# Weight quantisation prologue of an FFN-attention-FFN kernel: the loads for the mean scan move from ScalarE's queue to SyncE's, and the scale is folded and spread by TensorE instead of through DRAM

## What is computed

```python
def _weight_quant(w):
    scale = 1.0 / jnp.clip(jnp.mean(jnp.abs(w)), 1e-05)
    wq = jnp.clip(jnp.round(w * scale), -1.0, 1.0) / scale
    return w + jax.lax.stop_gradient(wq - w)
...
gate = jax.nn.silu(_bitlinear(x, w_gate))      # w_gate, w_up: 4096 x 1024
up = _bitlinear(x, w_up)
return _bitlinear(gate * up, w_down)           # w_down: 1024 x 4096
...
x = x + 0.5 * _L0_ffn_ref(_layernorm(x, axis=-1), w_gate, w_up, w_down)
x = x + _L0_attn_ref(_layernorm(x, axis=-1), w, u, mix_k, mix_v, mix_r, Wk, Wv, Wr, Wo)
x = x + 0.5 * _L0_ffn_ref(_layernorm(x, axis=-1), w_gate, w_up, w_down)
```

## Time and profile before

| | us |
|---|---|
| median of 2 timed runs | 8868.89 (8834.52 and 8903.26) |
| profiled execution, its own time | 8818.1 |
| its span on the slowest core (core 3) | 8816.5 |
| spans of the eight cores | 8726.9 to 8816.5 |
| TensorE, VectorE, ScalarE busy, core 3 | 3563.4, 2656.1, 1360.8 |

### The profile page before, as it was taken

One profiled execution on the slowest core, in us unless ns is written; L12 is line 12 of the kernel. 1 busy time (PEld: TensorE's weight loads), 2 busy tenths in 40 slices (PEclk: granted clock), 3 DMA queues, 4 the chain that ended last, 5 costly groups with the idle time before them and its releaser, 6 DMA issues.

```text
span 8816.5 us, 50500 instructions; the slowest of 8 cores (8726.9 to 8816.5 us)
## 1 busy us (share of the span) xinstructions
PE 3563.4 (40%) x15872; PEld 1586.1 (18%) x15872; DVE 2656.1 (30%) x2719; ACT 1360.8 (15%) x2012; POOL 687.6 (8%) x572
## 2 busy tenths in 40 slices
PE   0000435342464435342464435342464435442464
PEld 0000112131121112131121112131121112231121
DVE  0312131275302131275302132275302132275302
ACT  1221101021110101022110101021110101021110
POOL 0000101000110101000110101000110101000110
PEclk9999978776898778766798778766798778766797
DMA  7799432500243333501243322501243332501243
GB/s 171 205 229 197 132 85 90 129 1 29 85 115 91 122 85 93 124 1 37 80 122 86 124 82 93 122 1 38 82 118 86 124 85 92 119 1 48 80 121 96
DMA packets 1010045, 842.29 MB, mean 96 GB/s; under 512 B 639865, under 2 KB 902012, under 8 KB 990076
## 3 DMA queue, kind: packets, MB, share of 16 engines
q1 hardware_dynamic: 970768, 620.94, 28.4%
q10 hardware_dynamic: 29676, 167.79, 5.2%
q0 software_dynamic: 9344, 50.34, 2.2%
HBM read 536.90 MB, written 167.77 MB: 80 GB/s over the span
## 4 chain that ended last, share of the span: by engine, by line
PE 31%; DVE 24%; DMA 19%; SPq 11%; ACT 10%; issue 5%; DVEq 0%; ACTq 0%; POOL 0%; POOLq 0%
PE psA L552 11%; PE psA L559 10%; SPq L60 9%; DMA dslab<-scr_dT 9%; PE psA L654 7%; DVE s2v L593 3%; ACT gate_w L568 3%; DMA scr_hq<-hqb 3%; ACT u_w L571 3%; PE psA L818 2%; DVE hqi L621 2%; DVE hqb L624 2%; DMA mbat<-Wu 2%; DVE xkb L791 1%; DVE oh L899 1%
## 5 line engine op out<-in xcount | busy, mean ns | idle before, releaser
L552 PE MATMUL psA<-gslab,xqT 128*128 128x512 bf16 x4096 | 1003.0, 389 | 2164.6 <-DMA uslab<-scr_uT 1505.8
L654 PE MATMUL psA<-dslab,hqT 128*128 128x512 bf16 x4096 | 1084.4, 417 | 1919.6 <-DMA dslab<-scr_dT 1918.5
L577 POOL TENSOR_TENSOR hbuf<-gate_w,u_w 128x512 f16<-128x512 f32 x512 | 648.3, 1266 | 6529.2 <-ACT u_w L571 6529.2
L559 PE MATMUL psA<-uslab,xqT 128*128 128x512 bf16 x4096 | 975.2, 381 | 0.0
L552 PEld LDWEIGHTS psA<-gslab,xqT 128*128 128x128 bf16 x4096 | 379.2, 99 | 2763.3 <-issue 2389.3
L654 PEld LDWEIGHTS psA<-dslab,hqT 128*128 128x128 bf16 x4096 | 401.0, 105 | 2601.5 <-issue 2297.1
L593 DVE TENSOR_REDUCE s2v<-hbuf 128x4 f32<-128x16384 f16 x16 | 275.5, 17216 | 1276.5 <-POOL hbuf L577 1276.5
L666 DVE SCALAR_TENSOR_TENSOR xres<-psA,dsc,xres 128x1024 f32<-128x1024 f32 x64 | 77.7, 1277 | 1882.4 <-PE psA L654 1882.4
L568 ACT ACTIVATE gate_w<-psA,gsc 128x512 f32<-128x512 f32 x512 | 351.9, 687 | 1758.8 <-PE psA L559 1758.6
L559 PEld LDWEIGHTS psA<-uslab,xqT 128*128 128x128 bf16 x4096 | 403.9, 99 | 494.6 <-issue 20.2
L418 DVE TENSOR_SCALAR lnv<-lnv 128x4 f32<-128x4 f32 x24 | 4.1, 170 | 1415.7 <-ACT xqb L408 1415.7
(11 more groups left out here) (209 smaller groups left out, 3133.4 us busy)
## 6 DMA issues: line engine op xcount, KB each, us to landing
gslab<-scr_gT SPq DMA_DIRECT2D x128, 1024.0 KB, 5.4
uslab<-scr_uT SPq DMA_DIRECT2D x128, 1024.0 KB, 7.9
dslab<-scr_dT SPq DMA_DIRECT2D x512, 256.0 KB, 2.9
scr_hq<-hqb ACTq DMA_DIRECT2D x64, 1024.0 KB, 3.9
xres<-x SPq DMA_DIRECT2D x4, 4096.0 KB, 13.6
wbat<-Wd SPq DMA_DIRECT2D x8, 2048.0 KB, 26.7
mbat<-Wd ACTq DMA_DIRECT2D x8, 2048.0 KB, 8.7
mbat<-Wg ACTq DMA_DIRECT2D x8, 2048.0 KB, 10.0
```

Of the source, the lines that this page charges most:

```text
L552: inst = nc.tensor.matmul(psum(bk_g, IW), ap2(xqT[alt], ct * TTILE + sub * P, P), ap2(gslab[sb_], ct * IW, IW), start=(ct == 0), stop=(ct ...
L559: inst = nc.tensor.matmul(psum(bk_u, IW), ap2(xqT[alt], ct * TTILE + sub * P, P), ap2(uslab[sb_], ct * IW, IW), start=(ct == 0), stop=(ct ...
L577: G.inc(nc.gpsimd.tensor_mul(ap2(hbuf, sub * II + iw * IW, IW), gate_w[sb_][:], u_w[sb_][:]))
L654: inst = nc.tensor.matmul(psum(sub * NCW + cw, CW), ap2(hqT[hb], sub * P, P), ap2(dslab[hb], cw * CW, CW), start=(ic == 0), stop=(ic == NI ...
```

## The change

Three things change in the prologue. The mean scan's load is put on qtern, a queue that SyncE issues, and the wait for a free mbat buffer is SyncE's too. In scale_of the four DMAs go: TensorE sums acc over the partitions by a 1x1 product with a column of ones, ScalarE scales the sum out of PSUM, and a second product with a row of ones spreads the mean and its reciprocal to all partitions, from where VectorE copies them to wsc. The rest (qm, rowbuf, two DRAM scratch tensors, the flag do_rl, which was always true) is removed with them.

```diff
-        qm = DmaQ(nc, ctx, "qm", nc.scalar, k=4)
...
             if mb_guard[b]:
-                nc.scalar.wait_ge(S.sem, mb_guard[b])
-            tok = qm.put(ap2(mbat[b], 0, BN),
-                         win[nb * BW_ * P:(nb + 1) * BW_ * P, :])
-            qm.wait(S, tok)
+                nc.sync.wait_ge(S.sem, mb_guard[b])
+            tok = qtern.put(ap2(mbat[b], 0, BN),
+                            win[nb * BW_ * P:(nb + 1) * BW_ * P, :])
+            qtern.wait(S, tok)
...
             V.wait(V)
-            nc.scalar.wait_ge(V.sem, V.c)
-            if sc_prev["t2"] is not None:
-                qm.wait(nc.scalar, sc_prev["t2"])
-            t1 = qso.put(bass.AP(scr_red.tensor, 0, [[1, P], [1, 1]]), acc[:])
-            sc_prev["t1"] = t1
-            qso.wait(nc.scalar, t1)
-            t2 = qm.put(rowbuf[0:1, :],
-                        bass.AP(scr_red.tensor, 0, [[P, 1], [1, P]]))
-            sc_prev["t2"] = t2
-            qm.wait(S, t2)
-            if sc_prev["t3"] is not None:
-                qso.wait(S, sc_prev["t3"])
-            S.wait(S)
-            S.inc(nc.scalar.activation(ap2(obat, 0, P, 1), rowbuf[0:1, :],
-                                       ACT.Copy, accum_out=sca[0:1, 0:1],
+            TE.wait(V)
+            TE.inc(nc.tensor.matmul(psum(7, 1, 1), acc[:], onescol[:],
+                                    start=True, stop=True))
+            S.wait(TE)
+            S.inc(nc.scalar.activation(sca[:1, 0:1], psum(7, 1, 1), ACT.Copy,
                                        scale=1.0 / float(RR * CC2)))
...
             V.inc(nc.vector.reciprocal(sca[:1, 1:2], sca[:1, 0:1]))
             V.wait(V)
-            nc.scalar.wait_ge(V.sem, V.c)
-            t3 = qso.put(bass.AP(scr_sca.tensor, 0, [[2, 1], [1, 2]]),
-                         sca[0:1, 0:2])
-            sc_prev["t3"] = t3
-            qso.wait(nc.scalar, t3)
-            t4 = qm.put(wsc[:, 2 * widx:2 * widx + 2],
-                        bass.AP(scr_sca.tensor, 0, [[0, P], [1, 2]]), slow=True)
-            qm.wait(V, t4)
-            qm.wait(S, t4)
-
+            TE.wait(V)
+            TE.inc(nc.tensor.matmul(psum(7, 2), onesrow[:], sca[:1, 0:2],
+                                    start=True, stop=True))
+            scale_guard[0] = TE.c
+            V.wait(TE)
+            V.inc(nc.vector.tensor_copy(wsc[:, 2 * widx:2 * widx + 2],
+                                        psum(7, 2)))
+            V.wait(V)
```

More of the change, by code:

```diff
@@ L217, in build_nc @@
         red = sbt0("red", [P, 48])
-        rowbuf = sbt0("rowbuf", [1, P])
         sca = sbt0("sca", [1, 2])
@@ L221, in build_nc @@
         qg = DmaQ(nc, ctx, "qg", nc.sync, k=4)
-        qm = DmaQ(nc, ctx, "qm", nc.scalar, k=4)
[L223 to L229, removed]
+        ALLQ.append(qg)
+        wlist = [(2, wd_in, scr_d, scr_dT, C, II),
+                 (0, wg_in, scr_g, scr_gT, II, C),
+                 (1, wu_in, scr_u, scr_uT, II, C)]
         def nbat(RR, CC2):
@@ L233, in build_nc @@
         mean_sdone = {}
+        scale_guard = [0]
         mb_guard = [0, 0]
@@ L237, in build_nc @@
         bb_guard = [None, None]
-        sc_prev = {"t1": None, "t2": None, "t3": None}
         def mean_batch(oi, win, RR, CC2, nb):
@@ L262, in scale_of @@
             V.wait(S, mean_sdone[oi][NB - 1])
-            if sc_prev["t1"] is not None:
-                qso.wait(V, sc_prev["t1"])
+            V.wait(TE, scale_guard[0])
             V.inc(nc.vector.tensor_reduce(acc[:],
@@ L289, in scale_of @@
             V.wait(V)
-            nc.scalar.wait_ge(V.sem, V.c)
-            t3 = qso.put(bass.AP(scr_sca.tensor, 0, [[2, 1], [1, 2]]),
-                         sca[0:1, 0:2])
-            sc_prev["t3"] = t3
-            qso.wait(nc.scalar, t3)
-            t4 = qm.put(wsc[:, 2 * widx:2 * widx + 2],
-                        bass.AP(scr_sca.tensor, 0, [[0, P], [1, 2]]), slow=True)
-            qm.wait(V, t4)
-            qm.wait(S, t4)
+            TE.wait(V)
[6 more added lines that the diff above has]
+            V.wait(V)
+        relayout_pend = []
         prev_tr = [None, None, None]
-        relayout_pend = []
         def relayout_block(scr_nat, scr_T, RR, cb):
@@ L311, in relayout_block @@
                                  ap2(trow[b], 0, RR))
-        for oi, (widx, win, scr_nat, scr_T, RR, CC2, do_rl) in enumerate(wlist):
+        for oi, (widx, win, scr_nat, scr_T, RR, CC2) in enumerate(wlist):
             NB = nbat(RR, CC2)
@@ L318, in build_nc @@
             nxt0 = wlist[oi + 1] if oi + 1 < len(wlist) else None
-            NBn = nbat(nxt0[4], nxt0[5]) if nxt0 is not None else 0
             scale_of(oi, widx, RR, CC2)
@@ L323, in build_nc @@
             BN = BW_ * CC2
+            NBn = nbat(nxt0[4], nxt0[5]) if nxt0 is not None else 0
             vdone = {}
@@ L374, in build_nc @@
                 pend.pop(0)()
[L375 to L382, removed]
+            qso.wait_all(nc.sync)
+            relayout_pend = [
+                (lambda sn=scr_nat, st=scr_T, rr=RR, cb_=cb:
+                 relayout_block(sn, st, rr, cb_))
+                for cb in range(CC2 // P)]
+        for em in relayout_pend:
+            em()
         barrier()
```

## The result

Eleven timed runs of the changed kernel have a median of 8651.0 us, ten of the kernel before 8831.0; the ratio is 0.9799, with a 95% interval of 0.9765 to 0.9834. The gain is clear; whether it is over 2% is not. The direction was right, the size was not.

What follows compares the result with a forecast made beforehand. Transfers bound the prologue: M and R1 by one load at a time, R2, R3 and T by the DMA engines. Gains of 88 + 15 + 2 = 105 us off 8852 gave 8747 us, range 8665 to 8830.

Steps and rivals of the forecast that it cites:

- M and R1, 88 us: Prologue stages M and R1: mean loads queued ahead hold 329 GB/s, so R2 begins at 283 us instead of 371.
- 15 us in it for the first scale: Before R1: the first scale's 15 us on the path go with TensorE, counted inside the 88 us.
- R2 by the queue, 15 us: Stage R2: rounds stay 29.4 us, the end pause falls from 27 to 12 us; 247 us against 262.
- The scale, 2 us each by TensorE: The prologue's three scales: each takes 2 us (range 1 to 5) by two matmuls; the first took 16.4 before.
- The second and third are worth nothing by themselves: Second and third scales: no gain of their own, since SyncE issues transposes throughout and its queue ends these stages.
- R3, 2 us: Stage R3: loses the last mean load and the third scale's small DMAs, saving 2 us out of 225.
- The base: Whole kernel before: 8852 us, average of the profiled run and two timed runs, from which the gain was subtracted.
- Rival 3: Prologue: DMA engines are the only limit to 858 us; 205 us saved, 8647 us, chance 0.08.
- Rivals 1, 2 and 4: 1: R2 takes gain back, 8833, chance 0.13; 2: R2 loads delay transposes, 8907, 0.05; 4: rate not held, 8822, 0.06.

Runs made afterwards that it cites:

- e2: Changed kernel with the old scale through DRAM, so only the mean loads' move to SyncE's queue; against the kernel before: mean span -94 us, ratio 0.9881.
- e1: Kernel before with only the new scale on TensorE, mean loads left on ScalarE's queue; against the kernel before: mean span -75 us, ratio 0.9929.
- e11: Changed kernel plus a 128 x 4-byte write to DRAM behind each of R3's eight stores; against the kernel before: mean span -42 us, ratio 0.9945.
- e8: Changed kernel with VectorE held before the third scale until Wg's third transpose landed, no DMA added; against the kernel before: mean span -165 us, ratio 0.9809.
- e3: Changed kernel with mean loads back on ScalarE's queue, each issued one batch ahead; against the kernel before: mean span -142 us, ratio 0.9834.
- e13: Changed kernel plus eight small writes to DRAM in R1, where no transposes run; against the kernel before: mean span -39 us, ratio 0.9955.
- e4: Changed kernel with the third scale (Wu) alone through DRAM as before; against the kernel before: mean span -144 us, ratio 0.9824.
- e12: Changed kernel plus eight small reads in R3, each 128 pieces of 8 bytes; against the kernel before: mean span -174 us, ratio 0.9781.
- e16: The changed kernel itself, measured again in a later series; against the kernel before: mean span -167 us, ratio 0.9797.

## Why the prediction was wrong, step by step

- **M and R1, 88 us: right, but not by the queue alone.** R2 was to begin at 283; it begins at 284 on the middle core, with 301 and 308 GB/s for the 329 assumed. The sum had 15 us in it for the first scale. Beside queued loads that scale would have taken 43 us, and without the new one R2 begins at 319 (e2). The chain of M in the changed kernel shows loads of 9.8 us, two in flight:

```profile
109.66 9.84 DMA mbat<-Wd
...
123.87 10.46 DMA mbat<-Wd
```

- **R2 by the queue, 15 us: right in size, not in its place.** With the scale already new (e1), moving the loads takes R2 from 221 to 204 in one execution, to 218 in the other. The sum took it from the pause at the end, 27 to 12 us. That pause falls from 28 to 8 by the scale alone (e1) and to 4 with both; what the queue adds to e1 is mostly in the rounds, from 213 to 199 us in one execution and to 212 in the other. The size is thus partly luck. The rounds did not grow: groups of four transposes take 20 to 27 us on core 7 of the changed kernel, against 24.3 to 37.1:

```profile
290.23 21.46 SPq L60 DMA_TRANSPOSE trow<-scr_d  x4
...
314.24 26.84 SPq L60 DMA_TRANSPOSE trow<-scr_d  x4
```

- **The scale, 2 us each by TensorE: right.** From the reduction to the first rounding pass it is 2.7 us on core 7 for the first scale, where it was 16.4:

```profile
160.66 0.17 DVE L260 TENSOR_REDUCE acc<-red 128x1 f32<-128x16 f32 x1 [71.87 <-ACT obat L249]
...
163.34 2.35 DVE L321 TENSOR_SCALAR qbat<-wbat,wsc 128x4096 f32<-128x4096 f32 x1 [0.46 <-DMA wbat<-Wd]
```

- **"The second and third are worth nothing by themselves": wrong, and this is the step that failed.** Its reason was that SyncE goes on issuing transposes through both, and that "these stages end when SyncE's queue ends". R2 didn't end so: the rows had SyncE pausing for 27 us until ScalarE's last store landed, and the chain to that store began with the second scale, 34.7 us long, on ScalarE's own queue. The scale alone is worth 75 us (e1) where its share of my sum was 15: 30 us in R2, of which some 20 are this wait, and 34 in R3. In R3 the chain does run through SyncE, and there the second mistake counts: small DMAs don't only wait, they hold others up (e11, 16 us each). The second scale needed 34.7 us where the first, with nothing beside it, needed 16.4; I took this only for the small DMAs waiting for the large ones.
- **R3, 2 us: wrong.** It gained 43. Of these, some 10 are in rounds 1 to 4, which is within the scatter, and 34 in rounds 5 to 8. That the small DMAs cost something beside rounds 1 to 4 is likely: those took 84 us, against 57 in e8 with VectorE nearly as late and no small DMA. The 34 us in rounds 5 to 8 go with either half alone (e1, e2), and their cause stays open.
- **The base.** I took R3 and R2 from core 3, the slowest, and the time from an average of three runs, 8852; the median of ten is 8831. So the miss of 96 us in the time is 75 us of gain and 21 of base.
- **The rivals.** Rival 3 named the right size (8647, chance 0.08) for a reason that doesn't hold: R2 runs at 275 to 283 GB/s, not 329, and R3 at 203 to 256. Rivals 1, 2 and 4 did not happen. By the Trainium skill, page DMA: Bandwidth & Descriptors, section Queues, rings and completion order, each DMA engine goes round between the queues that have work; I had held this against the change. No loss of that kind is seen: e3, with the mean loads on a queue of their own, is 25 us slower than with all in line, not faster, with an error of some 9 us.

## What to carry to other kernels

Before a wait is called hidden, follow the chain to the end of its stage: the queue with the most work need not be the one that ends it. A DMA that writes tiny pieces to DRAM is priced by what it does to all other transfers of its core as well as by who waits for it: here 16 us each for 512 bytes (e11). Fold over partitions with a product with ones on an idle TensorE (0.2 to 0.6 us), and keep DRAM out of it. Where a stage is bound by the DMA engines, cut the table by stretch down to a few microseconds: a busy share near 1 at 26 GB/s is a stall that an average over the stage hides. And a low mean share of the DMA engines isn't room by itself: with the same 25 MB in one place of the main part it took 7930 us, in another 7887, where 7875 is the changed kernel's.

## What the hardware showed that I had not expected

- 128 pieces of 4 bytes written to DRAM slow plain 2 MB loads on another queue from 377 to 120 GB/s for 18 us (e13), and a load and a transpose to 26 GB/s for 10 us (e4). The same number of 8-byte pieces read costs nothing measurable (e12).
- Two queues with the same bytes are not better than one: -142 us with the mean loads on ScalarE's queue (e3), -167 on SyncE's (e16).
- The same four small DMAs of a scale take 16 to 19 us with little beside them and 43 beside queued 2 MB loads (e2, first scale).
- In a stage bound by transfers, VectorE's first pass 47 us after the start instead of 10 changed the end by nothing (R3 150 us against 159 and 163), as four loaded buffers were worked off in a burst. The first four rounds, without its stores beside them, took 57 us instead of 74, the last four 93 instead of 83.
